# Moving the relative-key product of an attention step from behind the second pair of score matmuls to behind the first

## What is computed

```
xn = _layernorm(x, axis=-1)
r = jnp.arange(S)
idx = jnp.clip(r[None, :] - r[:, None], -M, M) + M      # M = 128, 257 relative positions
rpk = rel_k[idx]
rpv = rel_v[idx]
content = jnp.einsum('bhqd,bhkd->bhqk', q, k)
relative = jnp.einsum('bhqd,qkd->bhqk', q, rpk)
scores = (content + relative) / jnp.sqrt(jnp.float32(hd))
w = jax.nn.softmax(scores, axis=-1)
out = jnp.einsum('bhqk,bhkd->bhqd', w, v) + jnp.einsum('bhqk,qkd->bhqd', w, rpv)
...
g = _silu(_L0_ffn_ref(xn, L0_ffn_W1, L0_ffn_W2, L0_ffn_Wg, L0_ffn_bg))
x = x + s * g
```

## Time and profile before

| | us |
|---|---|
| median of 3 runs | 2553.29 (2551.48 to 2554.37) |
| the profiled execution's own time | 2557.0 |
| its span, first to last instruction | 2555.4 |
| TensorE busy | 2399.6 (94%), 14704 matmuls |
| DVE busy | 1864.6 (73%) |
| ACT busy | 1676.0 (66%) |
| POOL busy | 1031.4 (40%) |
| granted TensorE clock, mean | 0.973 of 2.4 GHz |

### The profile page before, as it was taken

The page is one execution under the profiler, slowest core; times in us unless marked ns, Lnnn a source line. Parts: engine busy times, 40 slices in busy tenths (PEclk is TensorE's granted clock), DMA queues, the critical chain, the costliest instruction groups (busy, mean ns, idle before and its releaser), DMA issues. The chain is left out here.

```text
span 2555.4 us, 47614 instructions
## 1 busy us (share of the span) xinstructions
PE 2399.6 (94%) x14704; PEld 1167.3 (46%) x14704; DVE 1864.6 (73%) x5113; ACT 1676.0 (66%) x3898; POOL 1031.4 (40%) x2491
## 2 busy tenths in 40 slices
PE   6837999999999999999999999999999998699998
PEld 3411444444444444444444444444444443566666
DVE  6658888888888888888888888888888881333333
ACT  4523777777777777777777777777777777221111
POOL 1233444444444444444444444444444436133332
PEclk8965999999999999999999999999999999899999
DMA  5668788777787777777777777777777752822221
GB/s 164 170 154 266 252 276 266 242 229 242 244 248 231 241 243 247 241 241 245 243 249 240 233 245 242 249 229 239 243 247 237 235 187 51 318 93 67 67 67 50
DMA packets 351154, 540.98 MB, mean 212 GB/s; under 512 B 30608, under 2 KB 259392, under 8 KB 350912
## 3 DMA queue, kind: packets, MB, share of 16 engines
q1 hardware_dynamic: 336880, 502.76, 63.6%
q0 software_dynamic: 14032, 35.24, 4.6%
HBM read 272.60 MB, written 269.43 MB: 212 GB/s over the span
## 5 line engine op out<-in xcount | busy, mean ns | idle before, releaser
L1097 DVE TENSOR_REDUCE part<-ps 128x1 f32<-128x512 f32 (+3 forms) x2048 | 1197.4, 589 | 328.9 <-PE ps L984 313.3
L1153 ACT ACTIVATE probs_T<-pst 128x512 f32<-128x512 f32 (+3 forms) x2048 | 1016.2, 523 | 369.3 <-PE pst L993 367.4
L984 PE MATMUL ps<-k_front,q_front 96*128 96x512 bf16 x2048 | 805.5, 394 | 26.2 <-DVE part L1095 1.9
L933 PE MATMUL pout<-probs_T,v_far 128*32 128x512 f32 (+3 forms) x4864 | 546.1, 535 | 0.9 <-ACT probs_T L1136 0.7
L847 POOL TENSOR_TENSOR left_T<-probs_T,left_mask 128x128 f32<-128x128 f32 x512 | 217.4, 427 | 604.1 <-ACT probs_T L1136 448.8
L984 PEld LDWEIGHTS ps<-k_front,q_front 96*128 96x128 bf16 x2048 | 197.3, 96 | 563.0 <-DVE part L1097 330.8
L993 PE MATMUL pst<-q_back,k_right 102*128 102x512 bf16 (+3 forms) x1024 | 350.9, 343 | 5.0 <-ACT probs_T L1153 4.1
L993 PE MATMUL pst<-q_back,k_left 102*128 102x512 bf16 (+3 forms) x1024 | 352.4, 344 | 3.0 <-ACT probs_T L1153 1.8
L1166 ACT ACTIVATE band<-band,negm 128x384 f32<-128x384 f32 (+1 forms) x512 | 308.3, 602 | 0.1
L1095 DVE CUSTOM_DVE_ANT_0 band<-ps,band 128x256 f32<-128x256 f32 (+2 forms) x704 | 299.3, 425 | 0.0
L933 PEld LDWEIGHTS pout<-probs_T,v_far 128*32 128x32 f32 x4864 | 163.6, 108 | 225.4 <-issue 195.2
(11 more groups left out here) (160 smaller groups left out, 2256.2 us busy)
## 6 DMA issues: line engine op xcount, KB each, us to landing
rel_scores<-rel SPq DMA_DIRECT2D x128, 1024.0 KB, 8.3
band_probs<-band SPq DMA_DIRECT2D x128, 768.0 KB, 4.0
pwin<-band_probs SPq DMA_DIRECT2D x128, 512.0 KB
band<-rel_scores SPq DMA_DIRECT2D x64, 768.0 KB, 6.6
band<-rel_scores SPq DMA_DIRECT2D x64, 576.0 KB, 5.4
w<-in_w_dram SPq DMA_DIRECT2D x16, 1024.0 KB, 15.4
band<-rel_scores SPq DMA_DIRECT2D x64, 128.0 KB, 5.7
q_terms<-terms SPq DMA_DIRECT2D x48, 128.0 KB
```

The costliest lines, as they stand in the source:

```text
L933: return nc.tensor.matmul(pout[32 * g:32 * g + 32, c0:c1], values, probs, start=first, stop=False, skip_group_check=True)
L984: nc.tensor.matmul(ps1[u % 2][:, :], q_front[a.par][:, a.s * P:(a.s + 1) * P], k_front[a.par][:, u * CW:(u + 1) * CW], start=True, stop=Tr ...
L1097: ins = nc.vector.tensor_reduce(peak, src, AX_X, ALU.max)
L1153: ins = nc.scalar.activation(probs_T[t.s % 2][:, u * CW + c0:u * CW + c1], pst[u % 2][:, c0:c1], ACT.Exp, scale=SCALE)
```

## The change

Inside the loop over the four quarters of a step on TensorE, the block that issues the relative-key product is guarded by `u == 1` before and by `u == 0` after. It stands in the code behind the `ps` and `pst` matmuls of its quarter and behind `left_values`, and ahead of `key_values`. Its waits move with it: on the load of `q_front` (in the step with x.s = 0, which is p = 0), on ACT's copy of the product before (`r_evac`) and, at p = 5, on `norm_done`. Nothing is changed on the other engines, and no DMA is moved.

```diff
                         if u == 0 and ended.s == NB - 1 and ended.valid:
                             pe.wait_ge(left_ready, ended.count(16, 16))
                             left_values().then_inc(all_pv, 1)
-                        if u == 1 and x.valid:
+                        if u == 0 and x.valid:
 
                             if x.s == 0:
                                 pe.wait_ge(qf_in[x.par], x.count2(48, 48))
```

## The result

| | before | after |
|---|---|---|
| median of the runs, us | 2553.83 (4 runs, 2551.48 to 2556.22) | 2521.88 (4 runs, 2520.45 to 2522.24) |
| the profiled execution's own time, us | 2557.0 | 2521.55 |
| its span, us | 2555.4 | 2519.9 |

The changed kernel takes 0.987 of the time of before, 95% interval 0.9856 to 0.9885: 1.3% faster, clear of the noise, by 32 us between the medians and 35.5 us between the two profiled executions. The mean granted clock was 0.973 before and 0.972 after, so the clock has no part in it. The forecast was 35.5 us, which puts the profiled execution at 2521.5 and the median at 2518; the median came out 4 us higher.

What follows compares the result with a forecast made beforehand. A loop through TensorE and DVE was taken to bound each step; 0.69 + 0.46 + 0.21 + 0.09 - 0.28 = 1.17 us a unit, 35.5 us in all, gave a median of about 2518 us, range 2507 to 2536.

Steps and rivals of the forecast that it cites:

- The loop and the pause: Work between second and third `ps` lengthens every step; before the second `ps`, a TensorE pause of about 0.21 hides work.
- the first rival: The pause isn't usable: quarter 0 loses what quarter 1 gains, only p = 5 counts; +8 us, 2561; chance 0.06.
- The gain of a step: Product hidden at p = 0, 2, 3, 4 and 10 to 15; 0.115 us gained in each.
- p = 6 to 9: Product exceeds the pause; gain 0.07 each at p = 6 to 8, 0.09 at p = 9.
- p = 1: No pause as `left_values` fills quarter 0, no value products in quarter 1; gain 0.
- p = 5: Product waits for DVE's division, queuing second `ps` and `pst` behind it; loss 0.28 a unit, 29 times.
- DVE as the bound: DVE limits the third maximum, stopping half the gain at p = 4 to 9; 23 us, 2530; chance 0.12.
- a sign of being wrong: No DVE idle time left before the third maximum; at p = 10 it was 0.42, forecast to shrink by 0.12.
- The sum: Gains and loss over one unit of attention steps: 1.17 us, over 30 units 35.5 us.
- The load of `q_front`: At p = 0 the load is asked for about 0.65 earlier; 20 us if late each time, put at 0.
- the rival with no change: Within 5 us of 2553: `q_front` late at every p = 0, product costing a third of its slot; chance 0.04.
- The rule weighed: 512-column TensorE matmuls: the skill's 131 ns each, some 5 us more gain, against 0.22 kept; chance 0.01.

Runs made afterwards that it cites:

- the fastest variant above: The changed kernel with the product at p = 5 put behind the value products of quarter 1; 2496.15 us, ratio to the kernel before 0.9769.
- the last variant: The fastest variant above with the value products moved to quarter 2 behind its ps and pst in every step; 2711.75 us, 1.061 of the kernel before.

## Why the prediction was right, point by point

- *The loop and the pause.* Right. DVE's signal still sets the second `ps` at p = 0, 2, 3, 4 and 10 to 15, where it comes 0.058 to 0.059 behind the last maximum (0.057 to 0.058 before), so the product ahead of it takes nothing out of the path and the first rival fell; TensorE's own work sets it at p = 6 to 9, where it comes 0.085 to 0.100 behind.
- *The gain of a step.* 0.115 was forecast at the positions where the product is hidden; 0.108 to 0.113 was measured at all ten. The term, read from rounded starts, was 3% too large (0.112 in the averages): 0.03 a unit, 1 us.
- *p = 6 to 9.* Forecast 0.07, 0.07, 0.07 and 0.09, measured 0.09, 0.09, 0.08 and 0.10. The product does take 0.04 beyond the pause (0.025 at p = 9), as counted. What I left out is 0.02 on the path from the second `ps` to the value products. Together they are 0.49 apart in the kernel before, from 812.92 to the last of these rows of its timeline at p = 6:

```profile
813.14 0.23 PE L993 MATMUL pst<-q_back,k_right 102*128 102x128 bf16 x1
...
813.21 0.28 PE L1006 MATMUL prel<-rel_k,q_front 96*128 96x257 bf16 x1
...
813.41 1.06 PE L933 MATMUL pout<-probs_T,v_far 128*32 128x512 f32 x10
```

After, they are 0.36 apart (804.54 to 804.90). That is 0.13 and not 0.115. In the averages over 29 units this path shrinks by 134, 135, 126 and 126 ns at p = 6 to 9, against 113 where the product is hidden. 11 of these come from the second `pst`: in every kernel here that has both cases it starts 226 to 227 ns behind a second `ps` that had waited for DVE, and 215 behind one that followed the product without a wait. The other 10 at p = 6 and 7 lie between the second `pst` and the value products (0.12 instead of 0.11 less). Why is open for both. Together it adds 0.07 a unit over the four positions, 2 us.
- *p = 1.* Forecast 0, measured 0: from the first to the second `ps` 1.37 became 1.49, from the second to the third 0.56 became 0.44.
- *p = 5.* Forecast a loss of 0.28, measured 0.27. The wait in the trace is 0.62 where I had said about 0.7, since its idle time counts from the end of the matmul ahead of it. Undoing this step alone gave 8.6 us back, 29 x 0.27 = 7.8.
- *DVE as the bound.* I had called it a sign of being wrong if DVE had no idle time left before the third maximum. At p = 10 it has 0.30 left, but at p = 6, where it had 0.06, it has none:

```profile
805.90 0.39 PE L984 MATMUL ps<-k_front,q_front 96*128 96x512 bf16 x1
...
806.20 0.16 DVE L1055 TENSOR_TENSOR lm<-lm,rel_ends 128x12 f32<-128x12 f32 x1
806.33 0.42 DVE L1097 TENSOR_REDUCE part<-ps 128x1 f32<-128x256 f32 x1
```

The maximum still starts 0.43 behind its `ps`, as elsewhere, and the step gave its 91 ns, so nothing was lost there; but the change uses up all that DVE had to spare at p = 6, and at p = 5 of the fastest variant above DVE was the bound.
- *The sum.* Forecast 1.17 a unit, measured 1.21. From the first `ps` of step 18 to that of step 498 it took 1815.0 us before and 1778.1 after: 36.9 less, where 35.5 was forecast. What lies ahead of step 18 took 3.2 more in the later execution, and what lies behind 1.8 less; across the eight kernels traced, the stretch ahead of step 18 varies from 243.1 to 247.9 us. That the 35.5 us between the profiled executions were met exactly is luck; the size is not. The forecast of the median missed by 4 us because the earlier profiled execution lay 3.7 above the median of its runs and the later one at its median: a difference read from one execution carries that much.
- *The load of `q_front`.* Waited for twice, 28.7 us, against 28.4 before: the 20 us of the rival with no change did not arise.
- *The rule weighed.* Behind a 512-column `pst` the product starts 0.22 later (817.60 to 817.82), and at p = 6 the pause was too short for it, so the 131 ns of the Trainium skill (TensorE: Matmul & The Clock Gate, "Back-to-back issue gap") did not hold for this stream.

## What to carry to other kernels

Where two engines release each other, ask for each instruction on which side of the wait it stands: the same 0.11 us matmul cost 57 us when doubled inside the loop and 23 us when doubled ahead of the waiting instruction. Before moving an instruction forward, list its own waits; the one step in sixteen where it had to wait took back about a fifth of the gain, and giving that step a place of its own was worth another 19 us by the steps and 26 us by the medians. And count every loop through the shared buffers: taking work out of one and putting it into the next made the kernel 6% slower.

## What the runs showed of the hardware that was not expected

Going from a full-width matmul to the 32-column value products costs TensorE about 0.09 more than going to another full-width one: 0.31 from a 512-column `pst` to the value products (818.25 to 818.56) against 0.22 to the product (817.60 to 817.82). It is much the same behind a 128-column `pst` at p = 6 (0.15, 804.75 to 804.90, against 0.07, 813.14 to 813.21) and behind the product (0.20, 813.21 to 813.41, against 0.11, 804.43 to 804.54). The value products' fp32 inputs are not the reason: the fp32 transposes, full width, start 0.22 behind a 512-column `pst` too (825.72 to 825.94 in the kernel before).

From the end of DVE's last maximum to the start of the second `ps` that waits for it is 57 to 59 ns on average in every kernel here. The step lengths repeat from unit to unit with a standard deviation of 0 to 5 ns at nearly every position (15 at p = 5 of the kernel before, 27 at p = 13 of the last variant), so that a change of 0.01 in a step can be read from one trace, though the time of a whole launch moves by 13 us between executions (2549.90 to 2562.98 for the kernel before).
